# A stack of six graph-attention layers on one core: earlier row minima, and a context product made of halves

## The reference

```python
# layers 2 to 5, one step
q = x @ Wq.T + bq; kk = x @ Wk.T + bk            # 128 wide
scores = where(adj == 0, -1e10, q @ kk.T / sqrt(128))
attn = where(adj == 0, 0, softmax(scores))
ctx = (attn @ x) @ Wc.T
x = layer_norm(x + ctx) * gamma + beta
```

## Time and profile before

| | |
|---|---|
| median of 3 runs | 2490.63 us (2487.67 to 2492.85) |
| the profiled execution, its own time | 2490.31 us |
| its span, first to last instruction | 2488.5 us |
| PE busy | 2363.7 us, 95% |
| PE weight loads busy | 2179.7 us, 88% |
| POOL busy | 1843.6 us, 74% |
| DVE busy | 1695.1 us, 68% |
| ACT busy | 1576.8 us, 63% |
| granted TensorE clock | 0.99 of full speed |
| DMA queues | 7.6% of 16 engines |

### The profile page before, as it was taken

The page is one execution under the profiler, slowest core; times in us unless marked ns, Lnnn a source line. Parts: engine busy times, 40 slices in busy tenths (PEclk is TensorE's granted clock), DMA queues, the critical chain, the costliest instruction groups (busy, mean ns, idle before and its releaser), DMA issues.

```text
span 2488.5 us, 57766 instructions
## 1 busy us (share of the span) xinstructions
PE 2363.7 (95%) x21200; PEld 2179.7 (88%) x21200; DVE 1695.1 (68%) x4945; ACT 1576.8 (63%) x5515; POOL 1843.6 (74%) x2437
## 2 busy tenths in 40 slices
PE   6899999999999999999999999999999999999985
PEld 5789989989989989989889889889889889889874
DVE  4576676676776776776776776776776766766763
ACT  5576666666666666666666666666666666666642
POOL 4577777777777777777777777777777777777763
PEclk9999999999999999999999999999999999999997
DMA  3000000000000000000000000000000000000000
GB/s 145 22 25 31 19 29 31 18 29 31 18 29 27 22 29 27 21 31 27 21 31 25 22 31 22 25 31 23 25 31 23 25 31 22 25 31 12 14 9 13
DMA packets 38728, 68.66 MB, mean 28 GB/s; under 512 B 4400, under 2 KB 12848, under 8 KB 37936
## 3 DMA queue, kind: packets, MB, share of 16 engines
q1 hardware_dynamic: 38448, 64.97, 7.6%
HBM read 48.18 MB, written 16.78 MB: 26 GB/s over the span
## 4 chain that ended last, share of the span: by engine, by line
PE 65%; DVE 19%; ACT 7%; POOL 6%; issue 3%; DVEq 0%; DMA 0%; POOLq 0%; SPq 0%
PE value_bank L406 13%; PE qk_bank L398 12%; PE context_bank L559 8%; PE unit_bank L398 7%; PE qk_bank L512 5%; DVE y L868 5%; DVE y L849 4%; PE unit_bank L469 4%; POOL rstd L961 4%; ACT probs L639 4%; PE unit_bank L406 4%; DVE bn L857 3%; PE score_bank L543 3%; PE unit_bank L481 3%; PE score_bank L540 2%
## 5 line engine op out<-in xcount | busy, mean ns | idle before, releaser
L979 POOL TENSOR_TENSOR x<-y,rows 128x512 f32<-128x512 f32 x320 | 409.5, 1280 | 220.2 <-DVE y L868 218.6
L868 DVE TENSOR_SCALAR y<-y,mv,rstd 128x256 f32<-128x256 f32 x768 | 371.8, 526 | 280.9 <-POOL rstd L961 280.9
L661 ACT CAST xT_hi<-qk_bank 128x512 fp32r<-128x512 f32 x320 | 187.7, 587 | 432.1 <-PE qk_bank L512 432.1
L398 PE MATMUL qk_bank<-xT_hi,w_lo 128*128 128x256 f32 x1280 | 405.4, 317 | 53.5 <-DVE xT_lo L812 53.3
L985 POOL TENSOR_TENSOR x<-x,rows 128x512 f32<-128x512 f32 x320 | 413.4, 1292 | 25.1
L406 PE MATMUL value_bank<-w_lo,xT_hi 128*128 128x256 f32 x1280 | 393.9, 308 | 0.2 <-ACT v L679 0.2
L639 ACT ACTIVATE probs<-unit_bank,negmax 128x128 f32<-128x128 f32 x1024 | 365.5, 382 | 34.8 <-DVE negmax L779 34.8
L398 PE MATMUL qk_bank<-xT_lo,w_hi 128*128 128x256 f32 x1280 | 363.4, 284 | 0.0
L406 PE MATMUL value_bank<-w_hi,xT_lo 128*128 128x256 f32 x1280 | 361.7, 283 | 0.0
L398 PE MATMUL qk_bank<-xT_hi,w_hi 128*128 128x256 f32 x1280 | 361.2, 282 | 0.0
L406 PE MATMUL value_bank<-w_hi,xT_hi 128*128 128x256 f32 x1280 | 360.1, 281 | 0.0
(11 more groups left out here) (93 smaller groups left out, 6477.4 us busy)
## 6 DMA issues: line engine op xcount, KB each, us to landing
x0T<-xT_in SPq DMA_DIRECT2D x64, 256.0 KB, 3.0
x<-x_in SPq DMA_DIRECT2D x64, 256.0 KB, 3.0
out<-x_out SPq DMA_DIRECT2D x64, 256.0 KB, 2.2
adj<-adj_in SPq DMA_DIRECT2D x64, 128.0 KB, 2.1
late_weights<-w_in SPq DMA_DIRECT2D x2, 1024.0 KB, 7.4
rows<-rows_in SPq DMA_DIRECT2D x1, 1792.0 KB, 12.1
probs0T<-w_in SPq DMA_DIRECT2D x4, 256.0 KB, 3.9
x<-w_in SPq DMA_DIRECT2D x1, 1024.0 KB, 13.0
```

What stands on the lines that cost most here:

```text
L398: mm = pe.matmul(psum[:, n * G * N:(n + 1) * G * N], split(w, name, kd, at, at + P), flat(xT_half[:, kd]), start=kd == 0 and w is w_lo, st ...
L868: m = dve.tensor_scalar(y[:, r, g], y[:, r, g], mv[:, r, g, 0:1], rstd[:, r, g:g + 1], ALU.subtract, ALU.mult)
L979: pool.tensor_tensor(result(norm), y[:, NORM_AT[norm] % YS], row_of_each(f"gamma{layer}"), ALU.mult).then_inc(zg_ready, 1)
```

## The change

Two things are done.

1. The normalise of the join (layer 0 of a group) leaves the end of DVE's slot 3 and stands in slot 4 behind the row minima and the low half. On POOL, scale and shift of the group now stand ahead of the shift of the item. `x_ready` is therefore counted in another order (`RESULTS`).
2. The context of layers 2 to 5 is made of three products of halves in place of one f32 product. ACT's copies of `v` and `probsT` become high halves, and DVE gets two new instructions per item, `split_v` (128x512) and `split_probsT` (128x256). PE's waits for `v` and `probsT` become waits for the low halves, which DVE makes last. Layer 1 keeps the f32 product, with one buffer.

```diff
+RESULTS = [n for i in SLOTS for n in ([("group", due(i, 2))] if due(i, 2) is not None else []) +
+           ([("item", i - 2)] if item(i - 2) else [])]
 # PE
+            def wait_values_moved(i):
+                if item(i)[0] == 1:
+                    pe.wait_ge(v1_ready, item(i)[1] + 1)
+                else:
+                    pe.wait_ge(v_lo_ready, KEPT_AT[i] + 1)
+            def wait_probsT_moved(i):      # the same with probs1T_ready, probsT_lo_ready
 ...
             def project_v(i, g):
                 if g == 0 and NTH[i] > 0:
-                    pe.wait_ge(v_ready, NTH[i])
+                    wait_values_moved(ITEMS[NTH[i] - 1])
 ...
             def score(i):
                 if NTH[i] > 0:
-                    pe.wait_ge(probsT_ready, NTH[i])
+                    wait_probsT_moved(ITEMS[NTH[i] - 1])
 ...
             def context(i):
-                pe.wait_ge(probsT_ready, after(i))
-                pe.wait_ge(v_ready, after(i))
+                wait_probsT_moved(i)
+                wait_values_moved(i)
 ...
-                    mm = pe.matmul(context_bank[:, g * D:(g + 1) * D], probsT[:, ring(i), g], v[:, ring(i), g],
-                                   start=True, stop=True)
+                    for left, right in ((probsT_hi, v_lo), (probsT_hi, v_hi), (probsT_lo, v_hi)):
+                        mm = pe.matmul(context_bank[:, g * D:(g + 1) * D], left[:, ring(i), g], right[:, ring(i), g],
+                                       start=right is v_lo, stop=left is probsT_lo)
 # ACT
             def move_v(i):
                 act.wait_ge(v_in_psum, after(i))
-                act.copy(flat(v[:, ring(i)]), value_bank[:, :]).then_inc(v_ready, 1)
+                if NTH[i] >= RING:
+                    act.wait_ge(context_in_psum, after(i) - RING)
+                act.copy(flat(v_hi[:, ring(i)]), value_bank[:, :]).then_inc(v_hi_ready, 1)
 ...
 # DVE
+            def split_v(i):
+                dve.wait_ge(v_hi_ready, KEPT_AT[i] + 1)
+                dve.tensor_tensor(flat(v_lo[:, ring(i)]), value_bank[:, :], flat(v_hi[:, ring(i)]).bitcast(F32),
+                                  ALU.subtract).then_inc(v_lo_ready, 1)
+            def split_probsT(i):
+                dve.wait_ge(probsT_hi_ready, KEPT_AT[i] + 1)
+                dve.tensor_tensor(flat(probsT_lo[:, ring(i)]), score_bank[:, 0:G * N],
+                                  flat(probsT_hi[:, ring(i)]).bitcast(F32), ALU.subtract).then_inc(probsT_lo_ready, 1)
 ...
                     row_max(i - 1)
                 if item(i):
                     split_lo(i)
+                if (group := due(i, 1)) is not None:
+                    normalise(("group", group))
 ...
                     move_v1(i - 1)
+                elif item(i - 1) and not late_values(i - 1):
+                    split_v(i - 1)
                 if item(i - 2):
                     add_residual(("item", i - 2))
                     statistics(("item", i - 2))
                 if item(i - 1):
                     reciprocal_total(i - 1)
+                if item(i - 1) and late_values(i - 1):
+                    split_v(i - 1)
+                if item(i - 1) and item(i - 1)[0] > 1 and due(i, 2) is None:
+                    split_probsT(i - 1)
 ...
                 if item(i - 2):
                     normalise(("item", i - 2))
+                if item(i - 1) and item(i - 1)[0] > 1 and due(i, 2) is not None:
+                    split_probsT(i - 1)
                 if (group := due(i, 2)) is not None:
                     add_residual(("group", group))
                     statistics(("group", group))
-                    normalise(("group", group))
 # POOL
                 if (group := due(i, 2)) is not None:
                     find_rstd(("group", group))
+                    scale(("group", group))
+                    shift(("group", group))
                 if item(i - 2):
                     shift(("item", i - 2))
-                if (group := due(i, 2)) is not None:
-                    scale(("group", group))
-                    shift(("group", group))
```

More of the change, by code:

```diff
@@ L85 @@
 NORM_AT = {n: at for at, n in enumerate(NORMS)}
+RESULTS = [n for i in SLOTS for n in ([("group", due(i, 2))] if due(i, 2) is not None else []) +
+           ([("item", i - 2)] if item(i - 2) else [])]
+RESULT_AT = {n: at for at, n in enumerate(RESULTS)}
 def layer_and_group(norm):
@@ L171, in gnn_stack @@
         kT = sb("kT", [G, N])
-        v = sb("v", [RING, G, D])
+        v = sb("v", [G, D])
+        v_hi = sb("v_hi", [RING, G, D], F32R)
+        v_lo = sb("v_lo", [RING, G, D], F32R)
         probs = sb("probs", [RING, G, N])
-        probsT = sb("probsT", [RING, G, N])
+        probsT = sb("probsT", [G, N])
+        probsT_hi = sb("probsT_hi", [RING, G, N], F32R)
+        probsT_lo = sb("probsT_lo", [RING, G, N], F32R)
         SMALL = 4
@@ L249, in gnn_stack @@
         v_in_psum = sem("v_in_psum")
-        v_ready = sem("v_ready")
+        v1_ready = sem("v1_ready")
+        v_hi_ready = sem("v_hi_ready")
+        v_lo_ready = sem("v_lo_ready")
         scores_in_psum = sem("scores_in_psum")
@@ L256, in gnn_stack @@
         probsT_in_psum = sem("probsT_in_psum")
-        probsT_ready = sem("probsT_ready")
+        probs1T_ready = sem("probs1T_ready")
+        probsT_hi_ready = sem("probsT_hi_ready")
+        probsT_lo_ready = sem("probsT_lo_ready")
         context_in_psum = sem("context_in_psum")
@@ L349, in store @@
             def store(group):
-                sp.wait_ge(x_ready, NORM_AT["item", PERIOD * group + STEP * (LAYERS - 2)] + 1)
+                sp.wait_ge(x_ready, RESULT_AT["item", PERIOD * group + STEP * (LAYERS - 2)] + 1)
                 sp.dma_start(out[group // S][:, group % S], x_out[:, group % STORES]).then_inc(stored[group % STORES], 16)
@@ L506, in transpose_x @@
                 layer, group = item(i)
-                pe.wait_ge(x_ready, NORM_AT[source_of(i)] + 1)
+                pe.wait_ge(x_ready, RESULT_AT[source_of(i)] + 1)
                 if NTH[i] > 0:
@@ L520, in project_qk @@
                 project(qk_bank, xT_hi[:, ring(i)], xT_lo[:, ring(i)], parts).then_inc(qk_in_psum, 1)
+            def wait_values_moved(i):
[4 more added lines that the diff above has]
+            def wait_probsT_moved(i):
+                if item(i)[0] == 1:
+                    pe.wait_ge(probs1T_ready, item(i)[1] + 1)
+                else:
+                    pe.wait_ge(probsT_lo_ready, KEPT_AT[i] + 1)
             def project_v(i, g):
@@ L558, in context @@
                 for g in range(G):
-                    mm = pe.matmul(context_bank[:, g * D:(g + 1) * D], probsT[:, ring(i), g], v[:, ring(i), g],
-                                   start=True, stop=True)
+                    if item(i)[0] == 1:
+                        mm = pe.matmul(context_bank[:, g * D:(g + 1) * D], probsT[:, g], v[:, g], start=True, stop=True)
+                        continue
+                    for left, right in ((probsT_hi, v_lo), (probsT_hi, v_hi), (probsT_lo, v_hi)):
+                        mm = pe.matmul(context_bank[:, g * D:(g + 1) * D], left[:, ring(i), g], right[:, ring(i), g],
+                                       start=right is v_lo, stop=left is probsT_lo)
                 mm.then_inc(context_in_psum, 1)
@@ L689, in move_probsT @@
                 act.wait_ge(probsT_in_psum, after(i))
-                act.copy(flat(probsT[:, ring(i)]), score_bank[:, 0:G * N]).then_inc(probsT_ready, 1)
+                if item(i)[0] == 1:
+                    act.copy(flat(probsT[:, :]), score_bank[:, 0:G * N]).then_inc(probs1T_ready, 1)
+                else:
+                    act.copy(flat(probsT_hi[:, ring(i)]), score_bank[:, 0:G * N]).then_inc(probsT_hi_ready, 1)
             def split_first(name):
@@ L824, in move_v1 @@
                     dve.wait_ge(rows_loaded, 16)
-                dve.tensor_tensor(v[:, ring(i)], by_graph(value_bank, D), row_of_each("bo1"),
-                                  ALU.add).then_inc(v_ready, 1)
+                dve.tensor_tensor(v[:, :], by_graph(value_bank, D), row_of_each("bo1"),
+                                  ALU.add).then_inc(v1_ready, 1)
+            def split_v(i):
[6 more added lines that the diff above has]
+                                  flat(probsT_hi[:, ring(i)]).bitcast(F32), ALU.subtract).then_inc(probsT_lo_ready, 1)
             def add_residual(norm):
```

## The result

| | before | after |
|---|---|---|
| median | 2491.61 us (4 runs, 2487.67 to 2492.85) | 2535.45 us (4 runs, 2534.49 to 2537.27) |
| ratio | | 1.018, 95% interval 1.0162 to 1.0197 |
| forecast | | 2531 us, range 2488 to 2556 |
| span of the profiled execution | 2488.5 us | 2532.7 us |
| one period (median of PE's starts of slot 4's masks, steady state) | 37.50 us | 38.20 us |

What follows compares the result with a forecast made beforehand. PE, 95% busy, was taken as nearly full, with a 37.50 us period. Slot 0's 0.83 us loss less slot 3's 0.15 gain gives +0.68 per period; over about 61 periods 41.5 us, so 2490.3 + 41 = 2531 us, range 2488 to 2556.

Steps and rivals of the forecast that it cites:

- six products of halves: PE's context of layers 2 to 5: six products of halves take 0.71 us.
- slot 3, join's residual against slot 4: On DVE at the end of slot 3: the join's residual starts 0.44 us later against the start of slot 4.
- join's normalise, start and length: DVE in slot 4: starts at 2.16 and takes 0.73 us, with POOL having nothing left to do beside it.
- slot 4, transposes: PE in slot 4: the transposes start at 5.9 instead of 7.34, putting PE 1.44 us ahead.
- item's normalise: On DVE: starts at 7.87, not earlier than the 7.72 before, because POOL's shift of x_out delays the item's deviation.
- row minima, q and k of slot 0: Slot 0: DVE's row minima start at 8.52, PE's q and k at 9.60, keeping 0.26 of the 1.44 us.
- split_v, values of slot 0: Slot 0: DVE's split_v starts at 11.85; PE waits for it and starts the values at 12.58 instead of 11.75.
- faster rival: PE keeps its slot 4 lead: 2452 us without the v wait, 2375 with POOL also out of the way; chance 0.14.
- no-change rival: POOL's shift of x_out does not delay the item's normalise: period 37.46 us, time 2488 us; chance 0.09.
- rival of a change that does not do what it says: Three products cost what four passes did, losing slot 3's 0.15 us: 2540 us; counted within the forecast's 0.70.
- much slower rival: The join's normalise stays at 1.67 us and all behind comes 0.94 later: 39.1 us per period, 2589 us; chance 0.07.
- price of the product: On PE: context 0.85 and q and k 1.42 of 2.27 us; halves gain 0.14 to 0.15 us per item.

Runs made afterwards that it cites:

- e3: The changed kernel with POOL's shift of x_out and its store moved to slot 2 of the next period; 2489.38 us, ratio 0.9997 to the kernel before.
- e4: The changed kernel with ACT's copy of layer 2's values and DVE's split_v moved earlier inside slot 0; 2465.67 us, ratio 0.9900 to the kernel before.
- e5: The changed kernel with both moves, those of e3 and e4; 2420.79 us, ratio 0.9723 to the kernel before.
- e1: The kernel before with the reorder of DVE and POOL only, context still one f32 product; 2457.80 us, ratio 0.9872.
- e7: e1 with shift of x_out late and ACT's copy of layer 2's values earlier, no halves; 2402.83 us, ratio 0.9653 to the kernel before.
- e2: The changed kernel with the reorder taken back, so only the halves are left; 2598.58 us, ratio 1.0434 to the kernel before.

## Why the prediction was right

| step | forecast | measured |
|---|---|---|
| six products of halves | 0.71 | 0.71 in slot 3, 0.82 in slot 4, 0.92 in slot 1 (with a wait in it) |
| slot 3, join's residual against slot 4 | -0.72 | 1236.26 - 1237.01 = -0.75 |
| join's normalise, start and length | 2.16, 0.73 | 2.14, 0.74 |
| slot 4, transposes | 5.9 | 6.04 |
| slot 0 starts | not given; 5.9 and 0.44 for the transposes make 6.34 | 6.76 |
| item's normalise | 7.87 | 7.87 |
| row minima, q and k of slot 0 | 8.52, 9.60 | 8.52, 9.59 |
| split_v, values of slot 0 | 11.85, 12.58 | 11.82, 12.54 |
| slot 1 starts | 14.99 | 14.94 |
| period | 38.18 | 38.20 |
| time | 2531 | 2535.45 |

The mechanism is shown, not only argued: each of the two places, undone alone, moved the time by about what the chain says (e3: 46 us where 44 were expected, e4: 70 where 81 were), and undone together they moved it by the sum of the two, 115 us. The faster rival named the right condition: the low half of v early and POOL out of the way. e5, where both hold, is 2421 us, not the 2375 that I gave for it; its period is 36.27 where 35.6 was given. Most of the 0.67 us is missing in slot 4, which became 1.04 us shorter and not 1.44: the transposes came 0.14 later than forecast, and the next mask product waited some 0.26 for `probsT_lo`. Slot 1 lost 0.18 us to the wait for POOL, where the rival had 0. The no-change rival priced the shift of x_out alone, 2488, and e3 measured 2489. The rival of a change that does not do what it says is excluded by the 0.12 us that slot 3 gained. The much slower rival is excluded by the join's normalise at 0.74 us.

The price of the product was right as a sum and wrong in its parts. Before, the f32 context took 0.67 us to the start of q and k, and q and k took 1.60 (1212.31 to 1213.91), 2.27 together; the prediction gave the context 0.85 and q and k 1.42.

```profile
1212.31 0.47 PE L398 MATMUL qk_bank<-xT_hi,w_lo 128*128 128x256 f32 x1
```

After the change the context takes 0.70 and q and k 1.45, 2.15 together. So the six products are no cheaper than the f32 ones; the 0.12 us are won in q and k, which no longer stand behind an f32 product.

```profile
1231.37 0.28 PE L588 MATMUL context_bank<-v_lo,probsT_hi 128*128 128x256 f32 x1
...
1232.07 0.28 PE L411 MATMUL qk_bank<-xT_hi,w_lo 128*128 128x256 f32 x1
...
1233.52 0.28 PE L419 MATMUL unit_bank<-w_lo,headsT_hi 128*128 128x256 f32 x1
```

The prediction missed a wait: PE's start of slot 0 is held by the scores' wait for `probsT_lo`, made in slot 4 from 1243.20 to 1243.62. The transposes stand 0.72 us ahead of the mask product, where 0.44 is their own time and 0.46 stood before. The profile names no releaser there; that it is this wait follows from the kernel and from e1 and e7, which have no `probsT_lo` and stand at 0.46 and 0.47. The wait costs nothing in the changed kernel, since q and k wait for DVE later in the same slot; that later wait became 0.68 us where I had given about 1.2. In e5, where q and k no longer wait, it costs PE time. By PE's starts, slots 4 and 0 together lost 0.78 (forecast 0.83), slot 1 lost 0.05 (forecast 0) and slot 3 gained 0.12 (forecast 0.15). The first error covers most of the other two, so that the period came within 0.02 us is in part luck. The time rose by 44 us between the two profiled executions where 41 was forecast. The 60 periods from the first to the last start of slot 4 account for 42.5 of it; ahead of them the changed kernel is 1.8 us shorter and behind them 3.5 longer, where I had 0 to -2 for both ends. Why the end is longer was not taken apart.

In e4 I had a wait for POOL as a rival only, with an unbroken run of POOL as its reason, and worked the sum without it. The wait came, by way of the statistics that `split_v` pushes back. It makes slot 1 of e4 0.13 us longer than in the changed kernel; the period is 0.12 above the forecast, some 7 of the 12 us. The rest does not lie in the period.

## What to carry to other kernels

When engines run fixed queues, price an edit by walking one period instruction by instruction from a wait that stays put, and look for the next in-order neighbour that takes the gap: here 1.3 us won in one slot was spent within the next. Before adding work to an engine with room, look for instructions in the other queues whose result no engine waits for and that stand ahead of ones somebody does wait for; moving one of those was worth 46 us, where the halves in all four layers could bring 37 at best by the forecast's price (0.6 us in each of 61 periods). Splitting an operand moves the release of the next step to the last engine in the row. Here the copy and the split behind it, both moved ahead in the slot, were worth 70 us, but what it pushes back has to be priced too: in e4 and e5 it was the statistics that POOL waits for. A product's price is also to be read with the products behind it: here all of the gain lay in those.

## What the runs showed of the hardware

A normalise of two 128x256 tiles (L868, SBUF to SBUF) takes 0.73 to 0.74 us where POOL runs nothing long, and 1.67 to 1.68 us when a 128x512 POOL instruction had started 0.07 us ahead of it; this held before and in e2, and for the join it vanished in the changed kernel, where POOL is idle beside it. Tile by tile, the trace of the kernel before has three levels: 0.38 to 0.42 us with no long POOL instruction beside the tile, 0.69 to 0.70 when one of POOL's 128x256 products (0.62 us) had started 0.07 to 0.11 us ahead of it, and 1.34 to 1.35 behind the start of the shift of x_out, in all 60 cases. The changed kernel keeps the middle one, at the end of slot 0:

```profile
1250.48 1.31 DVE L913 TENSOR_SCALAR y<-y,mv,rstd 128x256 f32<-128x256 f32 x2
```
```profile
1250.40 1.23 POOL L1020 TENSOR_TENSOR probs<-probs,rtotal 128x256 f32<-128x256 f32 x2
```

DVE's subtractions from a PSUM bank took 0.68 us also beside POOL's long instructions (mean 678 ns over 256). The Trainium skill, "SBUF — State Buffer", section "Who interferes with whom", tells both cases apart in this way: `tensor_scalar` can enter a mode that takes the port pair shared with GpSimd, and a VectorE instruction outside these modes with at most one SBUF input does not contend with it. The trace agrees, with 1.67 against 0.74 us for the first and 0.68 us either way for the second.

The six products take 0.71 us behind other products of halves and 0.82 behind the f32 ones of slot 4; the 0.92 of slot 1 has a wait of q and k in it (0.80 in e4, where they do not wait there). The twelve products of q and k take 1.60 to 1.63 us directly behind an f32 context (slot 3 before, slot 4 of e7), 1.53 behind a wait, and 1.42 to 1.45 behind a context of halves.
